# First graph layer of a two-layer GNN kernel: neighbour table kept in fp32 and multiplied once, instead of three bf16 parts multiplied three times, with a ring of 128 tiles instead of 64

## The reference

```
h = relu(layernorm(x))
row = concat(src, nodes); col = concat(dst, nodes); ew = 1 for edges, 2 for self
reduced = segment_sum(h[col] * ew, row) / max(count(row), 1)
x = x + relu(concat(reduced, h) @ kernel + bias)            # first layer
h = relu(layernorm(x))
q, k, v of h[src], h[dst];  weights exp(clip(q.k/4)) per head, normalised over src
x = x + layernorm(segment_sum(weight * v, src) + h) * gamma + beta   # second layer
```

## Time and profile before

| what | before |
|---|---|
| median of the runs | 5896.75 us |
| span of the profiled execution | 5884.4 us |
| first layer's summing loop (first to last start of line 1001) | 220.9 to 3055.8 us |
| PE / DVE / ACT / POOL busy | 52 / 52 / 36 / 55 % |

### The profile page before, as it was taken

The page is one execution under the profiler, slowest core; times in us unless marked ns, Lnnn a source line. Parts: engine busy times, 40 slices in busy tenths (PEclk is TensorE's granted clock), DMA queues, the critical chain, the costliest instruction groups (busy, mean ns, idle before and its releaser), DMA issues. The chain is left out here.

```text
span 5884.4 us, 82972 instructions
## 1 busy us (share of the span) xinstructions
PE 3071.8 (52%) x19417; PEld 2269.0 (39%) x19417; DVE 3038.8 (52%) x8517; ACT 2089.2 (36%) x6025; POOL 3217.7 (55%) x3339
## 2 busy tenths in 40 slices
PE   4445445445445455354357555555555555555553
PEld 3324323334334333233234444444444444444442
DVE  7536446445345455354234555555555555555557
ACT  3233333433433333333344333333333333333333
POOL 3464464464564564554634555655555555555564
PEclk9556556556556556566557666666666666666665
DMA  2232232232222322322322333333333333333333
GB/s 80 63 82 53 70 80 55 73 79 55 76 72 56 81 68 57 84 62 61 87 57 68 101 103 100 106 101 102 104 101 105 102 101 105 101 104 103 100 105 63
DMA packets 245464, 490.01 MB, mean 83 GB/s; under 512 B 73156, under 2 KB 155197, under 8 KB 245022
## 3 DMA queue, kind: packets, MB, share of 16 engines
q0 software_dynamic: 153968, 371.50, 24.5%
q1 hardware_dynamic: 90350, 112.89, 6.9%
q10 hardware_dynamic: 704, 0.33, 0.0%
HBM read 468.15 MB, written 56.11 MB: 89 GB/s over the span
## 5 line engine op out<-in xcount | busy, mean ns | idle before, releaser
L533 POOL DMA_INDIRECT got<-hk_table,dst x1563 | 1561.2, 999 | 1325.5 <-PE bank L1003 647.5
L1513 POOL DMA_INDIRECT kv<-kv_table,dst_i x1611 | 1523.0, 945 | 1062.8 <-DVE wv_s L1554 611.4
L765 DVE TENSOR_TENSOR acc<-acc,bank 128x129 f32 x2187 | 634.2, 290 | 1250.2 <-remote 640.9
L1001 PE MATMUL bank<-got,oh 128*128 x2187 | 609.3, 280 | 1170.6 <-DVE acc L765 627.0
L1658 PE MATMUL bank<-q,ohT 128*128 x4833 | 757.8, 263 | 878.4 <-issue 574.6
L1572 DVE TENSOR_TENSOR acc<-acc,bank 128x136 f32 x1611 | 465.4, 289 | 1130.0 <-remote 1070.7
L1669 PE MATMUL bank<-wv_s,oh_f 128*128 128x136 f32 x3222 | 806.6, 401 | 255.5 <-issue 251.1
L1658 PEld LDWEIGHTS bank<-q,ohT 128*128 128x128 bf16 x4833 | 487.9, 101 | 1124.5 <-issue 1018.6
L1104 ACT ACTIVATE oh<-away 128x384 bf16<-128x384 bf16 x733 | 383.1, 523 | 1321.9 <-remote 784.1
L1669 PEld LDWEIGHTS bank<-wv_s,oh_f 128*128 128x128 f32 x3222 | 660.0, 282 | 344.0 <-issue 336.1
L1001 PEld LDWEIGHTS bank<-got,oh 128*128 128x128 bf16 x2187 | 239.9, 110 | 1369.2 <-issue 1317.5
(11 more groups left out here) (223 smaller groups left out, 3344.4 us busy)
## 6 DMA issues: line engine op xcount, KB each, us to landing
lane_r<-lane_of_slot SPq DMA_DIRECT2D x269, 192.0 KB
slots_by_bin<-sorted_chunk SPq DMA_DIRECT2D x637, 61.0 KB
kv<-kv_table,dst_i POOLq DMA_INDIRECT x1611
got<-hk_table,dst POOLq DMA_INDIRECT x1563
kv_table<-qkv SPq DMA_DIRECT2D x12, 512.0 KB, 2.9
hk_table<-hk POOLq DMA_DIRECT2D x6, 772.0 KB, 5.3
out<-o SPq DMA_DIRECT2D x12, 256.0 KB
xs<-in_x SPq DMA_DIRECT2D x3, 768.0 KB, 9.7
```

Source lines behind the costliest of these rows:

```text
L533: g.indirect_dma_start(out=got[:, (tile0[k] + t) % RING0, :], out_offset=None, in_=hk_d, in_offset=bass.IndirectOffsetOnAxis(dst0[:, k % 2 ...
L765: v.tensor_tensor(out=o, in0=o, in1=total0(u)[:, i * W0:(i + 1) * W0], op=ALU.add)\
L1001: t.matmul(o, w, row(2 * D, 3 * D + 1), start=True, stop=False)
L1513: g.indirect_dma_start(out=kv[:, r, i, :], out_offset=None, in_=kv_d, in_offset=bass.IndirectOffsetOnAxis(dst_i[:, t:t + 1], 0))\
```

## The change

The table row becomes 128 fp32 values (512 B). `got` becomes a ring of 128 tiles of 129 fp32 values, of which the gather writes the first 128; the last one is set to 1 once, by POOL, ahead of the first gather (new semaphore `s_ones`, for which PE waits before turn 1). The three bf16 matmuls of a piece become one fp32 matmul. The one-hot matrix `oh0` becomes fp32. The splitting steps on DVE, ACT and POOL go. The buffers of the first block (`hn`, `hT` and the whole of `hk`) lie in `got` until the gathers begin. A lot is now 7 tiles, and there are 20 gather semaphores.

```diff
-RING0 = 64
+RING0 = 128
-GLOT = 4
-GSEMS = 18
+GLOT = 7
+GSEMS = 20
-ROW = 3 * D + 2
-    hk_d = dram("hk_table", [NODE_SLOTS, ROW], BF16)
+    hk_d = dram("hk_table", [NODE_SLOTS, D], FP32)
-    got = sbp(sorting, "got", [P, RING0, ROW], BF16)
+    got = sbp(sorting, "got", [P, RING0, W0], FP32)
+    got_words = got[:, :, :].rearrange("p a b -> p (a b)")
+    in_got = lambda a, n: got_words[:, a * D:(a + n) * D].rearrange("p (n f) -> p n f", f=D)
+    xs0 = in_got(0, BINS)
+    hk_s = in_got(BINS, BINS)
...
-        oh0 = table("oh0", [OHR, G, P], BF16)
+        oh0 = table("oh0", [OHR, G, P], FP32)
...
-                for u in range(PAIRS):
-                    split_low(u)
...
+                for n0, n1 in pieces(BINS, LOT):
+                    g.wait_ge(s_hi, -(-n1 // 2))
+                    g.dma_start(hk_view[:, n0:n1, :], hk_s[:, n0:n1, :]).then_inc(s_hkw, 16)
                 g.wait_ge(s_hkw, 16 * LOTS)
+                g.memset(got[:, :, D:W0], 1.0).then_inc(s_ones, 1)
+                g.wait_ge(s_ones, 1)
...
-                            g.indirect_dma_start(out=got[:, (tile0[k] + t) % RING0, :], out_offset=None, in_=hk_d,
+                            g.indirect_dma_start(out=got[:, (tile0[k] + t) % RING0, 0:D], out_offset=None, in_=hk_d,
...
-                def split_rest(u):
...
-                        row = lambda a, b: got[:, s, a:b].rearrange("p a b -> p (a b)")
-                        t.matmul(o, w, row(2 * D, 3 * D + 1), start=True, stop=False)
-                        t.matmul(o[:, 0:D], w, row(D, 2 * D), start=False, stop=False)
-                        ins = t.matmul(o[:, 0:D], w, row(0, D), start=False, stop=True)
+                        ins = t.matmul(o, w, got[:, s, :].rearrange("p a b -> p (a b)"), start=True, stop=True)
...
+                t.wait_ge(s_ones, 1)
...
-                        a.activation(hk3[:, 2 * w % (2 * LOT):2 * w % (2 * LOT) + m, 0:D], hk, ACT.Copy)\
-                         .then_inc(s_hi, 1)
...
-                        a.activation(hk3[:, 2 * w % (2 * LOT):2 * w % (2 * LOT) + m, D:2 * D],
-                                     rest[:, w % 4, 0:m, :], ACT.Copy).then_inc(s_mid, 1)
+                        a.activation(hk_s[:, 2 * w:2 * w + m, :], hk, ACT.Copy).then_inc(s_hi, 1)
```

More of the change, by code:

```diff
@@ L157, in build @@
     tile_id = sbp(sorting, "tile_id", [P, TT], FP32)
-    got = sbp(sorting, "got", [P, RING0, ROW], BF16)
-    xs0 = got[:, :, :].rearrange("p a b -> p (a b)")[:, 0:2 * BINS * D].bitcast(FP32)\
-        .rearrange("p (n f) -> p n f", f=D)
+    got = sbp(sorting, "got", [P, RING0, W0], FP32)
[3 more added lines that the diff above has]
+    hk_s = in_got(BINS, BINS)
+    hn = in_got(2 * BINS, 4).rearrange("p (u i) f -> p u i f", i=2)
+    hT = in_got(2 * BINS + 4, 4).rearrange("p (u i) f -> p u i f", i=2)
+    assert (2 * BINS + 8) * D <= RING0 * W0
     s_zero = sem("s_zero")
@@ L331, in build @@
         s_hi = sem("s_hi")
-        s_rest = sem("s_rest")
-        s_mid = sem("s_mid")
-        s_lo = sem("s_lo")
+        s_ones = sem("s_ones")
         s_hkw = sem("s_hkw")
@@ L485, in _ @@
                 c.inc(g.memset(sel[:, :, :], 0.0))
-                c.inc(g.memset(hk3[:, :, 3 * D:ROW], 0.0))
                 iota(iota_i[:, :], pattern=[[1, INC]], base=0, channel_multiplier=0)
@@ L492, in _ @@
                                       channel_multiplier=1))
-                c.inc(g.memset(hk3[:, :, 3 * D:3 * D + 1], 1.0))
                 after(g, c)
@@ L766, in add @@
                          .then_inc(s_a0, 1)
-                def split_rest(u):
[L769 to L772, removed]
-                    v.scalar_tensor_tensor(out=rest[:, u % 4, 0:m, :], in0=acc[:, 2 * u:2 * u + m, 0:D], scalar=0.5,
-                                           in1=hk3[:, 2 * u % (2 * LOT):2 * u % (2 * LOT) + m, 0:D],
-                                           op0=ALU.mult, op1=ALU.subtract).then_inc(s_rest, 1)
-                def pair(u):
-                    if 0 <= u - 3 < PAIRS:
-                        split_rest(u - 3)
                 def bin_tables():
@@ L837, in _ @@
                 bases(0)
-                for u in range(4):
-                    pair(u)
                 v.wait_ge(s_more, 1)
@@ L1128, in pair @@
                         a.wait_ge(s_hk, w + 1)
-                        if 2 * w % LOT == 0 and 2 * w >= 2 * LOT:
-                            a.wait_ge(s_hkw, 16 * (2 * w // LOT - 1))
                         a.activation(acc[:, 2 * w:2 * w + m, 0:D], hk, ACT.Copy, scale=2.0)
-                        a.activation(hk3[:, 2 * w % (2 * LOT):2 * w % (2 * LOT) + m, 0:D], hk, ACT.Copy)\
-                         .then_inc(s_hi, 1)
-                    if 0 <= u - 4 < PAIRS:
-                        w = u - 4
-                        m = len(nodes(w))
-                        a.wait_ge(s_rest, w + 1)
-                        a.activation(hk3[:, 2 * w % (2 * LOT):2 * w % (2 * LOT) + m, D:2 * D],
-                                     rest[:, w % 4, 0:m, :], ACT.Copy).then_inc(s_mid, 1)
+                        a.activation(hk_s[:, 2 * w:2 * w + m, :], hk, ACT.Copy).then_inc(s_hi, 1)
                 a.wait_ge(s_wT, 1)
```

18 lines of the change are left out of this document (removed).

## The result

The changed kernel takes 6495.3 us (median of four runs, 6483.0 to 6513.6) beside 5891.7 us for the kernel before: ratio 1.1025, 95% interval 1.1004 to 1.1046. The forecast was 5620 us (range 5500 to 5740), so faster; it is 10% slower. The profiled execution took 6485.7 us.

What follows compares the result with a forecast made beforehand. No engine was the bound by busy time: gathers nearly filled something all instruction streams share, slowing the rest. 5884.4 - 294 (loop) + 14 (start) = 5604 us span, 5617 with 12.4 us to the median, stated as 5620 us, range 5500 to 5740.

Steps and rivals of the forecast that it cites:

- the one on the ring: Summing loop: the ring of 128 removes POOL's 36.5 us wait per turn, only sharing time with and without gathers out anew.
- the flaw: Stated condition for being wrong: the ring's wait was what gave the other engines time to catch up; no size given.
- Signs that it had named: Trace marks of being right: 4374 matmuls, POOL waiting for row numbers, turns near 197 us, slow issue to about 270 us.
- Gathers at 1.47 us each, whatever the row: POOL's first-layer gathers: price independent of row size, so 122 x 1.47 = 179 us for a full chunk.
- Fewer PE instructions, 23 us a turn: Summing loop: fewer listed PE instructions cut a piece beside gathers from 1.385 to 1.18 us, 294 us in all.
- Lots of 7, counted at nothing: Gather lots: PE waits at worst some 4.4 us a turn, hidden by POOL's lead; 56 us without that lead.
- fp32 on ACT and PE: One-hots and products: nothing on ACT; PE between 0.41 us more and 0.33 us less per group, counted as nothing.
- The slow rival: PE becomes the bound through fp32 products at half clock, +301 us, 6211 us; chance 0.10.
- The start: First block and chunk 0's gathers: 12 us saved by dropped splitting, 26 us lost to gathers in one go, +14 us.
- POOL sets the pace: Rival, summing loop: a turn lasts as long as its gathers, 179 us, total 5385 us; chance 0.25.
- Nothing moves: Rival, summing loop: a piece stays at 1.385 us and the turn at 220 us, total 5910 us; chance 0.15.
- the rule: Profile-record block pushes back on its producers rather than lose a record; offered as fitting the slowdown beside gathers, without a rate.

Runs made afterwards that it cites:

- experiment 2: Changed kernel with POOL waiting as for a ring of 64, fp32 and lots of 7 kept: held 5917.5 us (0.9936), free 0.9995 of the kernel before.
- experiment 4: Kernel before with a ring of 128, lots of 7 and the third bf16 part left out, no fp32: held 6561.3 us (1.1014), free 0.9880.
- experiment 5: Changed kernel with each lot of gathers waiting for a PE group of its own, spread over a turn: held 5613.8 us (0.9538), free 0.9870.
- held: Run condition, switched by something unknown, in which the kernel before takes 5885 to 5969 us and "remote" ends over a thousand us of waits.
- experiment 7: Changed kernel with POOL waiting after each lot of 7 gathers until it has landed: held 6320.1 us (1.0577), free 4837.1 us (1.0630).
- experiment 6: Changed kernel with each gather fetching rows for only 64 of its 128 slots: held 6582.3 us (1.1044), not run under free.
- free: The other run condition, in which the kernel before takes 4550 to 4553 us and no wait ends in "remote".
- experiment 1: Both kernels run again without edit: held 6488.3 us changed and 5900.8 us before; free 4496.5 us changed (0.9872).

## Why the prediction was wrong

*The step that failed* is the one on the ring: "It makes no gather cheaper. POOL then fetches a chunk in one go [...] so the time with and without gathers is only shared out anew." It took the 1.385 us of a piece beside gathers (and from it 1.18) as a property of the gathers. It was a mean over gathers that the ring's wait bound to PE's progress, in rows of up to 16 with pauses between them. In one go the gathers of a chunk leave PE a piece only every 2.27 us, and each turn got longer: 276.4 us from chunk to chunk against 225.1. Experiments 2, 4 and 5 show it from three sides: the wait put back takes the loss away, the ring (with lots of 7) brings it without any fp32, and gathers paced by PE's groups turn it into a gain. All of this holds under *held* alone. What does the harm once POOL is not bound to PE, how close its gathers stand or how far they run ahead, stays open (experiments 5 and 7). The prediction had seen such a row at the start, 64 gathers with the others nearly at a standstill, and reckoned with it there alone. It named the flaw as what would make it wrong, but gave it no chance and no price. By its own sum: 161 us of gathers do 71 pieces, the 100 left take 119 us, 280 us a turn where it wrote 197. Signs that it had named did come: 4374 matmuls of 0.42 us at the median, no wait of 30 us for PE inside a turn but long ones for DVE's row numbers, and slow issue until the gathers of chunk 0 end at 268 us (44 matmuls in the 46 us before, 195 in the 46 us after).

*Gathers at 1.47 us each, whatever the row.* Half right. The row's size hardly matters (952 ns at 512 B in the changed kernel, 945 ns at 1,024 B in the second layer), nor does the number of rows (experiment 6). But 1.47 us was 1.25 us and a share of the pauses, and the ring's wait, which made the longest of them, was what kept the others going.

*Fewer PE instructions, 23 us a turn.* Not found alone: with the ring's wait kept, 226.1 us against 225.1 (experiment 2). With pacing the turn takes 200.1 us and the whole 5613.8 us, close to the 197 and 5620 of the forecast, but there two things changed, and a paced kernel with three parts wasn't run, so how much of the 25 us is due to instructions stays open. That the total is so near the forecast is luck: the kernel is another one.

*Lots of 7, counted at nothing.* With the wait of a ring of 64 they cost 31 us under *free* (4551.2 less 4519.8). With the wait of 128 that wasn't measured apart.

*fp32 on ACT and PE.* Right for ACT, 523 ns before and after. PE waits 1121.3 us for `add`, so it isn't the bound. The prediction's support for it was misread too: in the earlier trace rows the granted clock is at half in two of the four windows, with 0.58 and 0.75 in the others. The slow rival came nearer in time (6211 us), but by a mechanism that experiment 4 excludes. What the Trainium skill says of four passes ("FP8 and Floating Point Precision", section "TensorE Precision Notes") decides nothing here: the loss is as large with two bf16 products as with one fp32 product (experiment 4).

*The start.* The first sum comes 2.0 us later, where 14 was reckoned. What follows was mis-sized: the first sum of chunk 1 comes at 540.9 us against 440.3, 101 us later and not some 26, as the row of gathers runs into turn 1.

*POOL sets the pace.* This rival is what happens under *free*: turns of 165 us, no pause (experiment 1). *Nothing moves* holds for the kernel of experiment 2.

On the Trainium skill's "NOTIFIC — the notification-queue block" (section "Overflow: three behaviours, one of which stalls the engine"): no run shows that block, and none was made without records. The prediction said that the rule names no rate; the section has one, 6.6 M records/s, for a measurement in which no overflow was seen, and no run here shows what it means for this kernel. That the waits called "remote" come and go with the condition fits something outside the program that holds every engine back, and no more than that is shown.

## What to carry to other kernels

A wait that looks like pure loss may be what lets the other engines go on: before it is removed, look at when the work behind it will then run and how close together, and at a stretch of the trace that already runs without it. Where gathers run far ahead, tie each lot to the consumer's progress and not only to free slots: the paced kernel is the best of all here under *held* (0.954) and as good as the changed one under *free* (0.987), while pauses that don't depend on PE gave back 7 of 51 us a turn. And compare kernels side by side, since the sign of this change hangs on a condition that moves the same program from 4552 to 5885 us.

## What the runs showed of the hardware

- The kernel before took 4552.4 us and 5884.8 us on one chip, and the changed kernel there 4496.5 us and 6488.3 us. In the changed kernel's traces most instructions are as long in both (`add` 290 ns, a gather of the second layer 945 ns, one of the first layer 944 ns at the median), and it is the idle times that differ. In the mean a gather of the first layer is even longer under *free*, 1043 against 952 ns.
- Under *held*, an unbroken row of gathers 1.25 us apart leaves PE one group in 16 us; under *free*, rows of 41 to 46 such gathers, and one of 142, leave a piece at 0.95 to 0.97 us.
- A gather of 64 rows of 512 B takes 910 ns and one of 128 rows 952 ns, in as many packets.
- Under *held*, a pause of 1.9 us after each 7 gathers ends the groups of 16 us and brings the first sum from 222.9 to 153 us, but gives back only 7 of 51 us a turn. Pauses that are bound to PE's progress (rows of up to 14 or 21 gathers) give all of the loss back.
